# Clearing a finished layer's semaphores inside the next layer's normalisation

## The reference

```
x = x + L0_xattn(layernorm(x), ctx, ctx, mask)     # 16 heads of 8, 257 keys
x = x + L0_attn(layernorm(x))                      # 16 heads of 8, 32 keys, v = k
x = x + L0_ffn(layernorm(x))                       # 16 experts, top 4 of grouped gates, and a shared one
x = x + L1_xattn(layernorm(x), ctx, ctx, mask)     # 16 heads of 64, 257 keys
x = x + L1_attn(layernorm(x))                      # 16 heads of 64, quantised to 8 bits at each step
x = x + L1_ffn(layernorm(x))                       # 128 -> 512 -> 512 -> 512 -> 128, silu and gelu
layernorm(x) = (x - mean) / sqrt(var + 1e-5)
```

## Time and profile before

| | |
|---|---|
| median of three runs | 2771.66 us (2770.66 to 2772.89) |
| the profiled execution, its time | 2771.93 us |
| its span, first to last instruction | 2770.2 us |
| PE busy | 2272.8 us (82%) |
| DVE busy | 1654.2 us (60%) |
| ACT busy | 1559.2 us (56%) |
| POOL busy | 460.4 us (17%) |
| DMA, mean | 33 GB/s |

### The profile page before, as it was taken

The page is one execution under the profiler, slowest core; times in us unless marked ns, Lnnn a source line. Parts: engine busy times, 40 slices in busy tenths (PEclk is TensorE's granted clock), DMA queues, the critical chain, the costliest instruction groups (busy, mean ns, idle before and its releaser), DMA issues. The chain is left out here.

```text
span 2770.2 us, 66495 instructions
## 1 busy us (share of the span) xinstructions
PE 2272.8 (82%) x19392; PEld 1626.9 (59%) x19431; DVE 1654.2 (60%) x5152; ACT 1559.2 (56%) x3838; POOL 460.4 (17%) x1102
## 2 busy tenths in 40 slices
PE   5999999979669988999999999993455025399997
PEld 3777777757546666777778777772134013244443
DVE  5877887857454444666665666666889986611100
ACT  5888888867412234655655565553679457442221
POOL 2444445423113310000000000000000030000000
PEclk9999999989779988999999999997888555599999
DMA  3222222200100001111111111100000000000001
GB/s 90 74 74 71 75 74 70 74 15 0 25 0 0 0 33 62 48 42 42 41 45 43 37 47 41 43 27 31 0 1 0 0 2 3 21 22 0 0 0 31
DMA packets 153174, 90.36 MB, mean 33 GB/s; under 512 B 34032, under 2 KB 151168, under 8 KB 152704
## 3 DMA queue, kind: packets, MB, share of 16 engines
q1 hardware_dynamic: 153088, 89.26, 11.0%
HBM read 68.24 MB, written 20.97 MB: 32 GB/s over the span
## 5 line engine op out<-in xcount | busy, mean ns | idle before, releaser
L666 ACT ACTIVATE a_PR<-a_SM,a_nmx 128x257 f32<-128x257 f32 x512 | 253.3, 499 | 4.0 <-issue 3.3
L1038 ACT ACTIVATE c_PR<-c_SM,c_nmx 128x257 f32<-128x257 f32 x512 | 253.3, 501 | 0.0
L962 PE MATMUL c_bs<-c_cT,c_QP 128*128 128x257 f32 x1024 | 247.8, 385 | 0.8 <-ACT c_QP L1026 0.8
L981 PE MATMUL c_bo<-c_PT,c_C 128*128 128x512 f32 x512 | 240.7, 592 | 2.0 <-DVE c_PT L1098 2.0
L1072 DVE CUSTOM_DVE_ANT_0 c_SM<-c_bs,c_MB 128x257 f32<-128x257 f32 x512 | 215.1, 423 | 17.0 <-PE c_bs L962 14.2
L713 DVE CUSTOM_DVE_ANT_0 a_SM<-a_bs,a_MB 128x257 f32<-128x257 f32 x512 | 187.9, 422 | 44.5 <-PE a_bs L534 38.6
L962 PEld LDWEIGHTS c_bs<-c_cT,c_QP 128*128 128x128 f32 x1024 | 185.5, 191 | 26.3 <-issue 1.7
L946 PEld LDWEIGHTS c_bq<-c_XNT,c_A 128*128 128x128 f32 x1024 | 137.5, 196 | 67.3 <-issue 64.1
L1044 ACT ACTIVATE c_OT<-c_bo 128x512 f32<-128x512 f32 x128 | 76.5, 598 | 173.1 <-PE c_bo L981 173.1
L1098 DVE COPY c_PT<-c_bp 128x512 f32<-128x512 f32 x128 | 88.5, 691 | 121.4 <-PE c_bp L970 121.4
L933 POOL TENSOR_TENSOR c_XL<-quarter,c_PR 128x16 f32<-128x16 f32 x128 | 27.8, 218 | 774.1 <-DVE c_PR L1082 774.1
(11 more groups left out here) (486 smaller groups left out, 5326.0 us busy)
## 6 DMA issues: line engine op xcount, KB each, us to landing
a_C<-in_ctx_dram SPq DMA_DIRECT2D x128, 128.0 KB, 2.1
ctxT_dram<-a_cT SPq DMA_DIRECT2D x128, 128.0 KB, 1.9
c_cT<-ctxT_dram SPq DMA_DIRECT2D x128, 128.0 KB, 2.2
c_C<-in_ctx_dram SPq DMA_DIRECT2D x128, 128.0 KB, 2.1
a_MK<-in_mask_Bx1xSxS_bk_dram SPq DMA_DIRECT2D x128, 32.1 KB, 1.9
X<-in_x_dram SPq DMA_DIRECT2D x4, 512.0 KB, 6.1
g_h<-in_L_ffn_h_w_dram SPq DMA_DIRECT2D x2, 1024.0 KB, 7.9
out_dram<-X SPq DMA_DIRECT2D x1, 2048.0 KB, 8.7
```

The lines of the kernel that those rows point to most:

```text
L666: nc.scalar.activation(PR[:, 1 - par, hg, :], SM[:, 1 - par, hg, :], ACT.Exp, bias=nmx[:, 1 - par, hg:hg + 1], accum_out=den[:, 1 - par, h ...
L962: nc.tensor.matmul(b_s[hg][:, 0:SK], QP[:, r // 4 % 2, r % 4, 4 * hg:4 * hg + 4, :], cT[:, r, :], start=True, stop=True).then_inc(s_ps, 1)
L981: last = nc.tensor.matmul(b_o[:, :], C[:, buf, c, :], PT[:, s.r % 2, c, :, :], start=(c == 0), stop=(c == 1))
L1038: nc.scalar.activation(PR[:, 1 - par, hg, :], SM[:, 1 - par, hg, :], ACT.Exp, bias=nmx[:, 1 - par, hg:hg + 1], scale=SCALE, accum_out=den[ ...
```

## The change

The block of `clear_semaphores` is gone. At a layer's end its semaphores only move from the list `LIVE` to the list `DONE`. The next layer's `phase_norm` block now has a list for GpSimd too: it clears what stands in `DONE`. The numbers are given back when that block has ended, so the normalisation's own semaphores use others. For the last layer the same clears stand in the block that stores the result. The first normalisation follows on `phase_setup`, which retires nothing, so its `DONE` is empty.

```diff
--- before.py
+++ after.py
@@ -74,22 +74,26 @@
 
 
 LIVE = []
-
-
-def clear_semaphores(nc):
-
-
-    with ExitStack() as ctx:
-        block = ctx.enter_context(nc.Block())
-
-        @block.gpsimd
-        def _(pool):
-            for s in LIVE:
-                pool.sem_clear(s)
-
-    for s in LIVE:
+DONE = []
+
+
+def retire_semaphores():
+
+    DONE.extend(LIVE)
+    LIVE.clear()
+
+
+def clear_retired(pool):
+
+    for s in DONE:
+        pool.sem_clear(s)
+
+
+def release_retired(nc):
+
+    for s in DONE:
         nc.release_semaphore(s)
-    LIVE.clear()
+    DONE.clear()
 
 
 class Step:
@@ -189,6 +193,10 @@
         @block.sync
         def _(sp):
             loads(sp)
+
+        @block.gpsimd
+        def _(pool):
+            clear_retired(pool)
 
         @block.vector
         def _(dve):
@@ -280,6 +288,8 @@
                     for r in range(4):
                         last = nc.tensor.transpose(tp[par][:, r * P:(r + 1) * P], xn[:, par, r, :], sh.ident[:, :])
                     last.then_inc(turned, 1)
+
+    release_retired(nc)
 
 
 def tile_stats(nc, dve, sh, t, done, value):
@@ -2397,7 +2408,7 @@
 
         def layer(phase, *weights):
             phase(nc, sh, *weights)
-            clear_semaphores(nc)
+            retire_semaphores()
 
         layer(phase_xattn0, ctx_1024, mask_Bx1xSxS2_bk1, L0_xattn_Wq, L0_xattn_bq, L0_xattn_Wk, L0_xattn_bk,
               L0_xattn_Wv, L0_xattn_bv, L0_xattn_Wo, L0_xattn_bo)
```

## The result

The changed kernel takes 2744.93 us (median of four runs, 2743.95 to 2747.15) against 2772.27 us before (four runs, 2770.66 to 2773.8): a ratio of 0.9903, 95% interval 0.9885 to 0.992. It is faster by 27.3 us (by the interval 22.2 to 31.9), where 21.8 were forecast.

The account below looks back on a forecast made before the run. Most of the kernel was held near TensorE's bound, but six layer ends serial on GpSimd's clears. Span 2770.2 less 21.8 us removed, nothing added, leaves 2748.4; with 1.7 more outside the span and 0.3 less for the median, 2749.9 us, range 2744.5 to 2754.5.

Parts of the forecast that it names:

- the seams: Five passages from a layer to the next normalisation, and one ahead of the store, where the whole core waits.
- rival C: TensorE's clock stays up behind shorter pauses at the first and third layer ends; 4.5 us gained each, 2741 us; chance 0.07.
- Removed, 21.8 us: Clear block with its barrier gone at six layer ends: 20.1 us at five, 1.7 us ahead of the store.
- What stays at a seam: Wait left before a normalisation's first step, layer's release plus start: 0.38 us at four layer ends, 0.65 at layer d_.
- 281 clears at 0.071 us, 20.0 us of the sum: Cross-check of the removed time: GpSimd's semaphore clears in the six clear blocks, 20.0 of 21.8 us.
- Six barriers, 1.8 us: Rest of the removed time beside the clears: a drain and a barrier per clear block, 0.3 us each.
- Cover of 13.8 us: GpSimd's free time in the first layer-end normalisation; the largest set of clears takes 5.2 us, so moving them costs nothing.
- Added, nothing: Clears running beside the normalisation's semaphore hand-overs: taken as no cost, upper bound 2.7 us from 62 hand-overs at 44 ns.
- rival A: Moved clears hold up the normalisation's chain of hand-overs: 2.7 us back at most, 2750 to 2752.6 us; chance 0.07.
- Rival B: An instruction load, hidden while engines stood still, ends last at each of six layer ends: 6 us back, 2755.9 us; chance 0.05.
- Not changed: the other engines' lists: Lists of engines other than GpSimd stay the same and weight loads move along with the normalisation; no time in the sum.

Follow-up runs that it names:

- the second pair of profiles: Both kernels run and profiled once more without any edit: changed 2746.28 us (ratio 0.9904), before 2774.28 us (ratio 1.0005 to itself).
- the padded ones: Changed kernel with 12 unused semaphore increments heading VectorE's list (2754.32 us, ratio 0.9932), or TensorE's and ScalarE's lists too (2760.82 us, ratio 0.9952).

## Why the prediction was right, and what it missed

The term that the change is about, the seams, was right. That the time fell into the range all the same has some luck in it: the 4.8 us that no term had brought it to 0.4 us from the range's lower end, and the range reached so low only for a part of rival C.

- *Removed, 21.8 us:* right in mechanism and size. The six seams gave 22.0 us. What stays at a seam, 0.38 us by the earlier trace rows, measured 0.31; at the fifth normalisation I had taken 0.65 from a slow barrier, which was 0.3 this time. Ahead of layer g_ it is 0.7, and that isn't the barrier: all engines are released at 2393.8, ScalarE and SyncE start at once, and VectorE alone 0.4 us later:

```profile
2393.90 1.28 ACT L255 ACT_TABLE_LOAD   x1 [10.42 <-PEq L2200]
2394.34 0.21 DVE L227 TENSOR_TENSOR g_n_small<-stats 128x32 f32<-128x32 f32 x1 [0.70 <-PEq L2200]
```

  All seven kernels with this code on VectorE show it (seam 1.00), and none of the others. What VectorE does in these 0.4 us isn't shown.
- *281 clears at 0.071 us, 20.0 us of the sum:* doubling them on the path made the seams 20.1 us longer and the median 19.1.
- *Six barriers, 1.8 us:* six idle blocks back in the seams lengthened these by 1.9 us.
- *Cover of 13.8 us:* right, tested on both sides of its end (10.4 us of clears cost nothing, 15.5 us cost 2.3).
- *Added, nothing (rival A up to 2.7 us):* right. The chain took 3.17 us with one set of clears beside it and with two. By the 26.3 ns per increment of the Trainium skill ("TensorE: Matmul & The Clock Gate", "The cost: per-tile semaphore tail") the estimate was 1.6 us. The trace shows nothing of it: the chain took 3.16 us with no clears beside it, so clears on GpSimd don't queue with VectorE's increments in that way here.
- *Rival B, a load of code that ends last:* not seen as described. Four of the five first instructions waited 0.3 us, and no instruction packet moved in the 0.7 us ahead of layer g_; the nearest one starts 0.65 us behind VectorE's first step.
- *Rival C, TensorE's clock:* partly, and not where I had put it. The step that failed is "Not changed: the other engines' lists", from which I concluded that the stretches keep their times. They lost 4.8 us in the profiled execution. In layer g_, the preparation of weights between the end of the normalisation and VectorE's first instruction of the main loop, before and after (windows, columns as above), the same 51 matmuls:

```profile
2432.20:2443.90 11.70, 9.74 (x51) 8.10 (x52) 0.00 (x0) 7.90 (x13) 0.00 (x0) 0.79 0.01 2
```

```profile
2408.90:2418.70 9.80, 7.71 (x51) 6.07 (x52) 0.00 (x0) 7.47 (x13) 0.00 (x0) 1.00 0.01 2
```

  The 1.9 us that this stretch lost are these, at a clock of 1.00 in place of 0.79. In the second pair of profiles it was not the clock: the transposes of g_'s weights took 6.5 us in both, but began 16.3 us behind the normalisation's first step before and 14.9 us in the changed kernel, which is all of the 1.4 us between the stretches. What TensorE waits for there is a load, 3.25 us and 1.59 us long:

```profile
2436.36 1.97 PE L2267 MATMUL g_b<-ident,g_w 128*128 128x128 f32 x8 [3.25 <-DMA g_s<-in_L_ffn_w_s_dram]
```

```profile
2408.17 1.97 PE L2277 MATMUL g_b<-ident,g_w 128*128 128x128 f32 x8 [1.59 <-DMA g_s<-in_L_ffn_w_s_dram]
```

  The changed kernel issues that layer's first load 0.45 us ahead of VectorE's first step, the kernel before 0.05 us. So up to 0.4 us of g_'s gain may be the late VectorE of the seam in front of it, counted there as a loss.
- *What neither the sum nor a rival had:* 12 barrier instructions fewer (18 on GpSimd) move all code behind them, and two loops of VectorE take 0.24 us a turn more or less by how many instructions lie ahead of them. In the changed kernel the loop at the end of layer d_ came out on the better side: 7.57 us in place of 8.67, 1.1 us of the 4.8. Layer b_'s loop was on its better side before and after, with 0.18 us of idle time a turn. That this is the place of code, and not the pause or the clock, is shown by the 12 increments. The Trainium skill ("Runtime: NRT & Kernel Launch", "Instruction fetch mechanics") has a taken branch out of the loaded window fetch by DMA; here the slower turns of layer b_'s loop came with no packet at all, so the mechanism is another, and I can't say which.
- *Still open:* what divides the kernels in g_. The stretch was 338.2 to 339.7 us in the seven kernels with the changed kernel's code on VectorE and 340.5 to 342.3 in the others, the padded ones with the same short seams among them; so the shorter pause isn't the cause, and the place of code is tied to it in a way that no run explains. With an idle block per seam, or six in front, c_ lost 6.6 to 6.9 us to the clock, and no kernel here tells what sets that off. The gain of 1 to 1.5 us in stretch b_ is not the change's: other kernels with the same seams and the same VectorE code took up to 122.8 us, more than before.

## What to carry to other kernels

A stretch in which the whole core waits for one sequencer's bookkeeping stands in no busy time; look at the idle time before the first instruction of a phase and at what ended it, and move such work beside any phase in which that engine has nothing to do. Its price is then a sum of counts, and this one held within 0.3 us. What is left over after such an edit, 5 us of 2770 here, may belong to nothing that was meant: pad the same number of instructions back at a place where nobody waits, and compare several kernels stretch by stretch, before giving it a cause.

## What the runs showed that I had not expected

Twelve semaphore increments that nobody waits for, at the start of one engine's list, made the kernel 6 to 8 us slower (0.2 to 0.3%). Loops on VectorE turn in 1.18 or some 1.4 us (layer d_) and with 0.18 or 0.42 us of idle time at the branch (layer b_) by the number of instructions ahead of them; the loop of layer d_ did so without exception in fourteen profiles. The same preparation of weights takes 16.7 or 23.6 us by TensorE's granted clock. And a semaphore clear, recorded at 44 ns, takes 0.071 us of GpSimd's time and delayed no step of the chain that ran beside it.
